# A 16-bit product in front of each pair of cross attention scores

## What is computed

```python
q = (input @ Wq + bq).reshape(b, tq, H, D).transpose(0, 2, 1, 3)
kv = (encoded_features @ Wkv + bkv).reshape(b, tk, 2, H, D).transpose(2, 0, 3, 1, 4)
k, v = (kv[0], kv[1])
scores = jnp.einsum('bhqd,bhkd->bhqk', q, k) / math.sqrt(D)
attn = jax.nn.softmax(scores, axis=2)
out = jnp.einsum('bhqk,bhkd->bhqd', attn, v)
```

## Time and profile before

| what | value |
|---|---|
| median of 3 runs | 1884.54 us (1882.66 to 1884.92) |
| the profiled execution | 1883.69 us, span 1881.9 us |
| mean granted TensorE clock over the span | 0.909 |
| cross attention (the eight-step slots of b = 4 to 7) | 1081.3 to 1366.0 us, 284.7 us |
| TensorE busy in it | 223.76 us, clock 0.84 |
| VectorE, ScalarE busy in it | 208.17 us, 190.32 us |

### The profile page before, as it was taken

How to read it: one execution, slowest core, us unless ns; L and a number is a source line. 1 busy time by engine, 2 the same in 40 slices (tenths; PEclk the granted TensorE clock), 3 DMA queues, 4 the chain that set the end, 5 groups by cost and what they waited for, 6 DMA issues and landing times. The chain is left out here.

```text
span 1881.9 us, 32646 instructions
## 1 busy us (share of the span) xinstructions
PE 1593.4 (85%) x11328; PEld 1155.5 (61%) x11328; DVE 1218.0 (65%) x2035; ACT 930.5 (49%) x1746; POOL 625.7 (33%) x863
## 2 busy tenths in 40 slices
PE   4889986858899997588888977887747999999996
PEld 2445443558899997233333332222247999999995
DVE  3566552444578886477777468777764777777773
ACT  1345452122156664145545657667711666666662
POOL 5444420010036654633344334333011233333321
PEclk8899998968899999689999988887855999999998
DMA  5222211121158885522212312222033677677763
GB/s 139 49 44 57 47 36 34 56 67 37 49 170 234 231 236 132 132 65 41 52 40 57 64 33 62 48 48 51 1 114 117 192 210 219 198 208 217 199 185 84
DMA packets 192834, 200.21 MB, mean 106 GB/s; under 512 B 33121, under 2 KB 167778, under 8 KB 192642
## 3 DMA queue, kind: packets, MB, share of 16 engines
q1 hardware_dynamic: 156578, 155.12, 28.0%
q0 software_dynamic: 36096, 43.04, 12.2%
HBM read 139.52 MB, written 22.54 MB: 86 GB/s over the span
## 5 line engine op out<-in xcount | busy, mean ns | idle before, releaser
L648 ACT ACTIVATE l1a_sb_probs<-l1a_s_ps,l1a_sb_kmax 128x512 f32<-128x512 f32 x256 | 173.0, 701 | 83.5 <-issue 52.2
L1668 PE MATMUL l1m_g_ps<-l1m_sb_rows_hi,l1m_sb_hi 128*128 128x256 f32 x736 | 209.2, 284 | 1.4 <-DVE l1m_sb_rows_lo L1550 1.4
L1668 PE MATMUL l1m_g_ps<-l1m_sb_rows_hi,l1m_sb_lo 128*128 128x256 f32 x736 | 208.9, 284 | 0.0
L1668 PE MATMUL l1m_g_ps<-l1m_sb_rows_lo,l1m_sb_hi 128*128 128x256 f32 x736 | 208.9, 284 | 0.0
L452 POOL DMA_DIRECT2D l1a_sb_kst<-l1a_sb_hi x256 | 125.7, 496 | 248.2 <-PE l1a_s_ps L768 197.6
L549 DVE TENSOR_REDUCE l1a_sb_mx<-l1a_s_ps 128x2 f32<-128x1024 f32 x128 | 154.0, 1219 | 62.2 <-PE l1a_s_ps L731 62.0
L583 DVE TENSOR_REDUCE l1a_sb_kmax<-l1a_s_ps 128x2 f32<-128x1024 f32 x128 | 153.0, 1217 | 41.1 <-PE l1a_s_ps L768 40.8
L654 ACT ACTIVATE l1a_sb_probs<-l1a_s_ps 128x1024 f32<-128x1024 f32 x128 | 128.0, 1023 | 88.3 <-PE l1a_s_ps L768 87.9
L768 PEld LDWEIGHTS l1a_s_ps<-l1a_sb_qst,l1a_sb_kst 49*128 49x128 f32 (+1 forms) x512 | 50.4, 197 | 176.2 <-issue 94.2
L549 DVE TENSOR_REDUCE l0a_sb_mx<-l0a_s_ps 128x2 f32<-128x256 f32 (+3 forms) x128 | 103.4, 821 | 80.1 <-PE l0a_s_ps L742 78.7
L768 PE MATMUL l1a_s_ps<-l1a_sb_qst,l1a_sb_kst 49*128 49x512 f32 (+1 forms) x512 | 131.0, 518 | 28.4 <-ACT l1a_sb_probs L648 23.7
(11 more groups left out here) (339 smaller groups left out, 4198.6 us busy)
## 6 DMA issues: line engine op xcount, KB each, us to landing
l1m_sb_raw<-in_l1m_w SPq DMA_DIRECT2D x184, 256.0 KB, 3.6
l0m_sb_raw<-in_l0m_w SPq DMA_DIRECT2D x96, 256.0 KB, 3.6
l1m_sb_raw<-in_l1m_w SPq DMA_DIRECT2D x23, 1024.0 KB, 6.4
l0m_sb_raw<-in_l0m_w SPq DMA_DIRECT2D x24, 512.0 KB, 4.7
l1a_sb_qst<-l1a_sb_hi SPq DMA_DIRECT2D x256, 32.0 KB, 2.1
l1a_sb_kst<-l1a_sb_hi POOLq DMA_DIRECT2D x256, 32.0 KB, 2.0
l0a_sb_qst<-l0a_sb_hi SPq DMA_DIRECT2D x128, 32.0 KB, 2.1
l0a_sb_kst<-l0a_sb_hi POOLq DMA_DIRECT2D x128, 32.0 KB, 2.1
```

Source lines behind the costliest of these rows:

```text
L648: ins = act.activation(probs[:, n % 8, e, :], at[:, e, :], ACT.Exp, bias=kmax[:, n % 4, e:e + 1], accum_out=zsum[:, n % 4, e:e + 1])
L1668: ins = pe.matmul(at, s, m, start=n == 0, stop=n == len(passes) - 1)
```

## The change

In a cross batch, and only there, `scores_by_key` issues one more product into the buffer as soon as it is free, before the two score products. It multiplies before_b (the stationary operand, 128 by 128) by ones_b, read four times over to make 512 columns, both bf16, and writes all 128 partitions of the buffer's first half. The first score product then starts its own accumulation in the same bank (start=True), so that nothing of the added product is left. There are 128 such products, one for each step S of b = 4 to 7. It is the first instruction behind the wait of `buffer_free`; nothing else is added, moved or taken away.

```diff
                 buffer_free(pe, "S", b, g, j)
                 c0, at = first_col(kt), buffer("S", b, g, j)
+                if cross:
+
+                    pe.matmul(at[:, 0, :], const["before_b"][:, :],
+                              const["ones_b"][:, :].unsqueeze(1).to_broadcast([P, T // P, P]), start=True, stop=True)
                 for e in range(2):
                     rows = slice(64 * e, 64 * e + (48 if cross else 49))
                     ins = pe.matmul(at[:, e, c0:T], kst[rows, p, kt * P:(kt + 1) * P], qst[rows, p, c0:T],
```

## The result

Seven runs of each kernel give 1884.92 us before (1882.66 to 1887.36) and 1890.17 us after (1887.5 to 1891.47). The ratio is 1.0026, with a 95% interval of 1.0015 to 1.0038: slower by a quarter of a per cent, some 5 us. The forecast was 1886, within 0.2%; the time lies inside the range, on its slow half, just past the bound that I had called "the same".

The account below looks back on a forecast made before the run. The prediction saw no engine as the bound alone: the cross attention was partly a chain through three engines, with TensorE losing its clock. +4.6 + 2.4 - 3.9 - 1.5 = +1.6 us gave 1886 by the median, range 1876 to 1897.

Parts of the forecast that it names:

- the same: Whole kernel: a measurement tells about 0.2%, 3.8 us, from no change; chance of the same 0.42.
- The price of a product: Added product before the scores: 0.33 us at full clock, between bounds 0.24 and 0.43, and 0.6 at 1.2 GHz.
- Slot 1: Cross attention, b = 4 to 6: some five products a slot on the path, 1.5 us each slot, +4.6 in all.
- Slot 3 and the plain steps: Cross attention: eight products fit under ScalarE's 10.70 us, so nothing; at 0.43 us each, 0.1 us a plain slot.
- The clock where it is surely held: Cross attention's plain slots, slot from 1275.5 and cold starts of slot 0: full clock regained, -3.9 us.
- At the pauses: Slot 2 of each cross batch and last slot 0: clock holds at some pauses, -0.3 us a place, -1.5 in all.
- Slot 0: Cross attention, three times: products on the second half's chain cost 0.8 us a slot, +2.4; cold starts save 0.3 each.
- The last stage: Behind the cross attention: bound by TensorE at clock 1.00, unchanged in length, merely starting later or earlier.
- Dearer products, pauses that still drop the clock: Rival: 0.43 us a product and the clock still falling at five pauses, +9.5 us, 1894; chance 0.24.
- Clock not held: Rival: the added product leaves about 91 us of the stage at 1.2 GHz, +17 us, about 1901; chance 0.10.
- Held at the pauses too: Rival: clock held at all five pauses and slot 0's second halves, 1876 to 1880, taken as 1878; chance 0.24.
- The drain at a change of tiling: Each added product: a tiling change drains TensorE, so the higher bound, 0.43 us, would hold for each.

Follow-up runs that it names:

- The halves: Changed kernel with two side by side products of 64 rows in place of the one of 128 rows, 512 columns each; 1877.3 us, 0.9964 of the kernel before.
- the second set of halves: Changed kernel with the side by side products of 64 rows issued twice in place of its one product; 1890.0 us, 1.0023 of the kernel before.
- e2: Changed kernel with the added product only in slots 0 and 1 of b = 4 to 6, 48 steps; 1892.0 us, 1.0034 of the kernel before.
- e1: Changed kernel with the added product only in slots 2 and 3 and all of b = 7, 80 steps; 1886.6 us, 1.0011 of the kernel before.
- e7: Changed kernel with an added product of 256 columns in place of 512; 1887.3 us, 1.0005 of the kernel before.
- e9: Changed kernel with side by side 64-row products, and products filling the pauses ahead of the projection and in slot 0; 1879.1 us, 0.9958 of the kernel before.
- e10: Changed kernel with no product before the scores, but products filling the pauses ahead of the projection and in slot 0; 1882.7 us, 0.9977 of the kernel before.
- e4: Changed kernel with two side by side 64-row products in place of the one of 128 rows; 1877.3 us, 0.9964 of the kernel before.

## Why the prediction was right, and where it wasn't

**The price of a product** was 0.32 us against 0.33, and at 1.2 GHz 0.56 against 0.6. Right, but for a reason that was half wrong. I had set the lower bound at 0.24 and put the difference down to one change of tiling. The halves cost 0.12, below that bound. The pair of scores has some 0.2 us around the 0.21 us that 512 columns add (0.32 less 0.21 for half of them, and the second set of halves), and the halves fit into it. That it is the loading of the scores' stationary operands that is hidden there is an inference: the loads stand at the pair's start, and no run separated them.

**Slot 1**, forecast +4.6 us for three, was +3.0 in the profiled execution, +0.7, +1.6 and +0.8. The walk put five products on the path; by 0.7 to 0.8 us at 0.32 each, two and a half were in two of the three slots. The excess in b = 5 is most likely time carried over from slot 0, whose low stretch of the clock ended 0.9 us before slot 1 began: in e2 the one slot 1 behind such a late stretch took 21.5 us, the other two 20.4. The busy slots' part by itself, e2, was 6 to 7 us over the kernel before, with what it cost the slots behind it.

**Slot 3 and the plain steps** are the term that failed: "nothing" was +0.4 us in each of five slots, +2.0. TensorE was busy 10.22 of 11.10, so there was cover by the sum, but the products come in front of the work that others wait for. The cover was reckoned against ScalarE's 2.68 us for two steps, in the sum over both steps; VectorE, at 10.56 of 10.70 us, had next to none, and it waited 0.4 us for scores that came later, as its lines above show. I had the cover going at 0.43 us a product and costing 0.1 (by the prediction's own terms, 4 x (2.72 - 2.68), nearer 0.2); it went at 0.32 and cost 0.4.

**The clock where it is surely held**: the same five slots and the one from 1275.5 were forecast at -3.0 and came to -2.0 with the +2.0 of price in them, so the clock gave about 4. Slots 3 showed 1.00 everywhere, as expected. **At the pauses** the clock still fell in every one of the five slots, for 3.4 us where it had been 6.8 or more. Apart from the slot from 1275.5, counted above, they gave -0.5, less than the -0.3 a place that I had. What a held clock is worth there was sized well: in e1, where it held over the pause of b = 4, slot 2 took 14.35 us against 16.2, for 1.7 forecast. The stage's clock, 0.92 forecast, was 0.91.

**Slot 0**: +2.4 for the products less 0.9 for the start is +1.5; +1.9 was measured. Since the same slot took 25.0 to 28.4 us in other profiles, this agreement is partly luck.

The sum was +1.6 and the profiled execution's stage +2.3. That it is so near is luck in part: slot 1 cost 1.6 us less than forecast and the plain steps 2.0 us more, the surely held clock gave 1 us more and the pauses less. The measured medians differ by 5; the profiled execution is the shortest of the changed kernel's. What the others lost can't be seen, but e1, e7 and e9 show one candidate of the right size, the low stretch of the clock over slot 0's products, and the lower mean clock of the longer runs fits it.

**The last stage** is not at 1.00 throughout, as the prediction has it: from 1367.3 to 1456.0 us before and 1371.8 to 1460.6 us now the clock was 0.50, slices 30 and 31 of the page. It made no difference here, as the stage took the same time in both.

**The rivals.** "Dearer products, pauses that still drop the clock" had the right shape, plain slots over 11 us and clock falls at all five pauses, and 1894. "Clock not held" was wrong for this product and right for the one-row product, at four times the price that I had for it. "Held at the pauses too", 1878, needed the pauses' own filling and came out at 1874 with the cheaper shape. The drain at a change of tiling, from the Trainium skill (TensorEngine Tiling (Array Packing), Key Properties), would by the prediction's working have made the price 0.43. The trace has 0.32, and the halves' 0.12 agrees that a change costs something, if it is the tiling that they save. The Trainium skill (TensorE: Matmul & The Clock Gate, A second HAM failure mode: psum-queue depth-cycling) also tells of frequent small pauses between groups of matmuls that let the clock swing. The plain steps of e10, at 0.85 with no long pause near, agree.

## What to carry to other kernels

A thinly used TensorE can lose half its clock inside a pipeline that another engine paces, and filler work can hold it; but the filler must be cheaper than its place can bear, so try it in the shape and tiling of the product behind it, and put it into the pauses that are there anyway. Busy share of a slot isn't cover: see which products others wait for, and in which order the filler stands to them. A second engine without slack, VectorE here, decides what the place can bear. And read the clock by place, not by mean: slot 0 of b = 5 took 25.0 us with 3.4 us at 1.2 GHz (e4) and 25.4 us with 13.7 us of it (before), while 3.4 us of it on the products at the head of a chain cost 1.7 us.

## What the runs showed of the hardware

- Two side by side 16-bit products of 64 rows and 512 columns in front of two side by side products of 48 rows, float32r, 512 columns: 0.12 us for the added pair. One product of 128 rows in the same place: 0.32 us; with 256 columns 0.21, with 8 columns 0.10.
- A product of 512 columns with 1 row takes nearly as long as one with 128 rows (0.32 us both at 2.4 GHz, 0.54 and 0.56 at 1.2), and the clock behaved quite differently: 0.63 over the stage against 0.91.
- TensorE can be busy for 17.76 of 17.76 us by the profile and stay at 1.2 GHz; in the one-row kernel the clock was 0.50 through all the slots from 1339.5 to 1436.6 us, with TensorE busy 96.25 of these 97.1 us.
- An instruction that hardly takes time can lower the clock: with the eight-column product the stage's clock was 0.72, without it 0.83.
